# Group norm of an attention block in token order: normalised x split in halves and turned by DMA instead of x transposed on TensorE

## The reference

```python
g = v.reshape(B_, H_, W_, G, C_ // G)            # G = 32 groups of 24 channels
m = jnp.mean(g, axis=(1, 2, 4), keepdims=True)   # per image and group: 196 tokens x 24 channels
s = jnp.var(g, axis=(1, 2, 4), keepdims=True)
xn = (g - m) / jnp.sqrt(s + eps)
qkv = xn @ qkv_w.T + qkv_b                       # plus two low-rank terms in q and v
attn = softmax(q k^T / 8 + rel_h + rel_w)        # 12 heads of 64 channels
out = x + (attn v) @ proj_w.T + proj_b
```

## Time and profile before

| | |
|---|---|
| profiled execution, device time | 3388.14 us |
| its span | 3386.3 us |
| mean granted TensorE clock | 0.991 |
| PE / DVE / ACT / POOL busy | 97% / 75% / 62% / 1% |
| mean DMA traffic | 111 GB/s |

### The profile page before, as it was taken

The page is one execution under the profiler, slowest core; times in us unless marked ns, Lnnn a source line. Parts: engine busy times, 40 slices in busy tenths (PEclk is TensorE's granted clock), DMA queues, the critical chain, the costliest instruction groups (busy, mean ns, idle before and its releaser), DMA issues.

```text
span 3386.3 us, 80119 instructions
## 1 busy us (share of the span) xinstructions
PE 3295.3 (97%) x31972; PEld 2129.3 (63%) x31972; DVE 2525.2 (75%) x5966; ACT 2095.0 (62%) x5651; POOL 35.7 (1%) x65
## 2 busy tenths in 40 slices
PE   5789999999999999999999999999999999999998
PEld 3556666666666666666666666666666666666664
DVE  5677777777777777777777777777777777777764
ACT  1466666666666666666666666666666666666664
POOL 0000000000000000000000000000000000000000
PEclk9799999999999999999999999999999999999999
DMA  4145555555555565554555655556555555555555
GB/s 127 29 88 113 121 105 114 111 115 116 121 110 106 116 114 110 126 123 100 118 109 109 122 121 107 114 111 113 115 121 113 103 117 113 109 128 121 99 107 107
DMA packets 1097275, 376.13 MB, mean 111 GB/s; under 512 B 922560, under 2 KB 1077184, under 8 KB 1096904
## 3 DMA queue, kind: packets, MB, share of 16 engines
q1 hardware_dynamic: 1081070, 333.63, 50.0%
q10 hardware_dynamic: 15834, 37.37, 3.8%
HBM read 86.60 MB, written 38.54 MB: 37 GB/s over the span
## 4 chain that ended last, share of the span: by engine, by line
PE 94%; DVE 2%; ACT 1%; issue 0%; DMA 0%; POOL 0%; SPq 0%; POOLq 0%; DVEq 0%
PE ring L541 51%; PE ring L608 17%; PE score L584 9%; PE o_ps L598 7%; PE ring L563 3%; PE ring L622 3%; PE ring L614 3%; ACT prob L667 1%; PE ring L627 0%; PE ring L548 0%; DVE split L774 0%; DVE row_max L754 0%; DVE rel_sb L747 0%; DVE split L766 0%; DVE rel_sb L741 0%
## 5 line engine op out<-in xcount | busy, mean ns | idle before, releaser
L541 PE MATMUL ring<-xn_hi,w_hi 128*128 128x392 f16 x3456 | 1143.5, 331 | 4.9 <-DVE xn_lo L824 4.9
L541 PE MATMUL ring<-xn_lo,w_hi 128*128 128x392 f16 x3456 | 1140.0, 330 | 0.0
L541 PE MATMUL ring<-xn_hi,w_lo 128*128 128x392 f16 x3456 | 1139.8, 330 | 0.0
L667 ACT ACTIVATE prob<-score,neg_max,exp_scale 98x196 f32<-98x196 f32 x1536 | 768.6, 510 | 253.2 <-DVE neg_max L758 245.7
L754 DVE TENSOR_REDUCE row_max<-score 98x4 f32<-98x784 f32 x384 | 373.2, 972 | 275.1 <-PE score L584 274.1
L774 DVE SCALAR_TENSOR_TENSOR split<-prob,row_inv,split 98x196 f16<-98x196 f32 x1536 | 545.1, 418 | 7.8
L541 PEld LDWEIGHTS ring<-xn_hi,w_hi 128*128 128x128 f16 x3456 | 342.3, 99 | 260.9 <-issue 8.4
L541 PEld LDWEIGHTS ring<-xn_hi,w_lo 128*128 128x128 f16 x3456 | 338.8, 98 | 237.0 <-issue 2.6
L541 PEld LDWEIGHTS ring<-xn_lo,w_hi 128*128 128x128 f16 x3456 | 339.0, 98 | 208.8 <-issue 2.5
L608 PE MATMUL ring<-o_hi,w_hi 128*128 128x392 f16 x1152 | 380.2, 330 | 1.4 <-DVE o_lo L783 1.4
L608 PE MATMUL ring<-o_lo,w_hi 128*128 128x392 f16 x1152 | 379.6, 330 | 0.0
(11 more groups left out here) (115 smaller groups left out, 4895.7 us busy)
## 6 DMA issues: line engine op xcount, KB each, us to landing
y_sb<-in_x SPq DMA_DIRECT2D x192, 196.0 KB
out<-y_sb SPq DMA_DIRECT2D x192, 196.0 KB
x_sb<-in_x ACTq DMA_DIRECT2D x31, 1176.0 KB
rel_q<-rel_sb SPq DMA_DIRECT2D x128, 122.5 KB, 2.3
stage<-in_L_conv_qkv_w SPq DMA_DIRECT2D x3, 2304.0 KB, 19.9
turned<-split SPq DMA_TRANSPOSE x384, 4.1
rel_q<-rel_sb SPq DMA_DIRECT2D x128, 24.5 KB, 1.9
v_tok<-v_split SPq DMA_TRANSPOSE x192, 3.4
```

The costliest lines, as they stand in the source:

```text
L541: last = T.matmul(ring[:, bank, 0:NT], w[:, c, 128 * j:128 * j + 128], xx[:, par, c, :], start=(c == 0 and part == 0), stop=(c == CT - 1 a ...
L667: last = A.activation(prob[:, head, half, :], score[0:HALF, head, TOK * half:TOK * half + TOK], ACT.Exp, bias=neg_max[:, k % 2, i:i + 1], ...
```

## The change

The norm is computed on `x_sb` in token order. VectorE sums each group of 24 channels (A, two halves: one image each), one G step averages over tokens by products with a constant 98x98 matrix (four products of 64 columns, f32), B subtracts the mean in place, ScalarE squares (U), VectorE sums the squares (D), a second G gives the variance, POOL the power of -0.5 on 128 values per partition, H multiplies in place. I and L write the high and the low part to `xs` (f16, tokens on partitions), and four DMA transposes a pair (XT) write `xn`, channels on partitions, with 112 rows for 98 tokens. The buffer `xs` also serves as `squares` and as the column copy of q, so all of its zeroing is at the start. X and M are gone, weights are turned without the stride of six, `yT` has one buffer, `y_sb` two, and the lists are written anew.

```diff
-GP = C // GROUPS // CT
+GP = C // GROUPS
...
-YS = 3
+YS = 2
...
 PE_ORDER = (
-    each("S", 0, 0) + each("P", 1, 10) + each("Z", 2, 5) + each("X", -1, 3, 4, 5) + each("V", 0, 0)
-    + each("S", 0, 1) + each("P", 1, 11) + each("K", 0, 1) + each("Y", 1, 0) + each("G", -1, 0)
-    + each("S", 0, 2) + each("P", 0, 0) + each("G", -1, 1) + each("V", 0, 1) + each("Y", 1, 1) + each("Z", 1, 0)
...
+    each("S", 0, 0) + each("P", 1, 10) + each("Z", 2, 5) + each("V", 0, 0) + each("K", 0, 1)
+    + each("S", 0, 1) + each("P", 1, 11) + each("G", -1, 1) + each("V", 0, 1) + each("Y", 1, 0)
+    + each("S", 0, 2) + each("P", 0, 0) + each("K", 0, 2) + each("Y", 1, 1) + each("Z", 1, 0)
+    + each("S", 0, 3) + each("P", 0, 1) + each("Y", 1, 2) + each("Z", 1, 1) + each("V", 0, 2)
+    + each("S", 0, 4) + each("P", 0, 2) + each("Z", 1, 2) + each("K", 0, 3) + each("Q", -1, 0)
+    + each("S", 0, 5) + each("P", 0, 3) + each("V", 0, 3) + each("Q", -1, 1)
+    + each("S", 0, 6) + each("P", 0, 4) + each("K", 0, 4) + each("Q", -1, 2)
+    + each("S", 0, 7) + each("P", 0, 5) + each("V", 0, 4) + each("Q", -1, 3)
+    + each("S", 0, 8) + each("P", 0, 6) + each("G", -2, 0) + each("Q", -1, 4, 5)
+    + each("S", 0, 9) + each("P", 0, 7) + each("K", 0, 5) + each("R", -1, 0) + each("Y", 1, 3) + each("R", -1, 1)
     + each("S", 0, 10) + each("P", 0, 8) + each("R", -1, 2, 3, 4) + each("V", 0, 5) + each("Y", 1, 4) + each("Z", 1, 3)
-    + each("S", 0, 11) + each("P", 0, 9) + each("K", -1, 0) + each("X", -2, 0, 1, 2) + each("Y", 1, 5) + each("Z", 1, 4))
+    + each("S", 0, 11) + each("P", 0, 9) + each("K", -1, 0) + each("Y", 1, 5) + each("Z", 1, 4))
...
 ACT_ORDER = (
-    each("Y", 2, 5) + each("X", -1, 3) + each("N", 0, 0) + each("X", -1, 4, 5) + each("T", 0, 0)
...
-    + each("X", -2, 0, 1, 2))
+    each("Y", 2, 5) + soft(0) + each("V", 0, 0)
+    + each("K", 0, 1) + each("P", 1, 11) + soft(1) + each("V", 0, 1)
+    + each("Y", 1, 0) + each("I", -1, 0) + each("N", 0, 2) + each("K", 0, 2) + each("T", 0, 2) + each("I", -1, 1)
+    + each("Y", 1, 1) + each("P", 0, 1) + soft(3) + each("Y", 1, 2)
+    + each("V", 0, 2) + soft(4) + each("K", 0, 3)
+    + each("Q", -1, 0) + each("P", 0, 3) + soft(5) + each("V", 0, 3) + each("LD", -2, 0)
+    + each("Q", -1, 1) + each("N", 0, 6) + each("K", 0, 4) + each("T", 0, 6)
+    + each("Q", -1, 2) + each("P", 0, 5) + soft(7) + each("V", 0, 4)
+    + each("Q", -1, 3) + soft(8) + each("Q", -1, 4)
+    + each("Q", -1, 5) + each("P", 0, 7) + each("N", 0, 9) + each("K", 0, 5) + each("T", 0, 9) + each("R", -1, 0)
+    + each("Y", 1, 3)
+    + each("R", -1, 1, 2) + each("N", 0, 10) + each("R", -1, 3, 4) + each("T", 0, 10) + each("V", 0, 5)
+    + each("Y", 1, 4) + each("U", -2, 0) + each("P", 0, 9) + each("N", 0, 11) + each("K", -1, 0) + each("T", 0, 11)
+    + each("U", -2, 1))
...
 DVE_ORDER = (
-    each("S", 0, 0) + each("Z", 2, 4) + each("X", -1, 3) + each("N", 0, 0) + each("T", 0, 0) + each("Z", 2, 5)
-    + each("X", -1, 4)
...
+    each("S", 0, 0) + each("Z", 2, 4) + soft(0) + each("V", 0, 0) + each("Z", 2, 5) + each("D", -1, 1)
+    + each("S", 0, 1) + each("G", -1, 1) + each("K", 0, 1) + each("P", 1, 11) + soft(1) + each("V", 0, 1)
+    + each("H", -1, 0)
+    + each("S", 0, 2) + each("H", -1, 1) + each("N", 0, 2) + each("K", 0, 2) + each("T", 0, 2) + each("L", -1, 0)
+    + each("S", 0, 3) + each("Z", 1, 0) + each("P", 0, 1) + each("L", -1, 1) + soft(3)
+    + each("S", 0, 4) + each("V", 0, 2) + each("Z", 1, 1) + soft(4) + each("K", 0, 3)
+    + each("S", 0, 5) + each("Z", 1, 2) + each("Q", -1, 0) + each("P", 0, 3) + soft(5) + each("V", 0, 3)
+    + each("S", 0, 6) + each("Q", -1, 1) + each("N", 0, 6) + each("K", 0, 4) + each("T", 0, 6) + each("A", -2, 0)
+    + each("S", 0, 7) + each("Q", -1, 2) + each("P", 0, 5) + soft(7) + each("V", 0, 4) + each("A", -2, 1)
+    + each("S", 0, 8) + each("Q", -1, 3) + each("G", -2, 0) + soft(8) + each("Q", -1, 4) + each("B", -2, 0)
+    + each("S", 0, 9) + each("Q", -1, 5) + each("P", 0, 7) + each("N", 0, 9) + each("K", 0, 5) + each("T", 0, 9)
+    + each("R", -1, 0)
+    + each("S", 0, 10) + each("R", -1, 1, 2) + each("N", 0, 10) + each("R", -1, 3, 4) + each("T", 0, 10) + each("V", 0, 5)
     + each("S", 0, 11) + each("Z", 1, 3) + each("P", 0, 9) + each("N", 0, 11) + each("K", -1, 0) + each("T", 0, 11)
-    + each("X", -2, 0, 1, 2))
+    + each("B", -2, 1) + each("D", -2, 0))
...
 SP_ORDER = (
     each("ST", 2, 4) + each("CB", 0, 0) + each("T", 0, 0)
+    + each("VT", 0, 0) + each("ST", 2, 5) + each("LY", 1, 0) + each("T", 0, 1)
+    + each("VT", 0, 1) + each("LY", 1, 1) + each("XT", -1, 0) + each("T", 0, 2)
+    + each("XT", -1, 1, 2) + each("ST", 1, 0) + each("XT", -1, 3) + each("T", 0, 3) + each("LY", 1, 2)
+    + each("VT", 0, 2) + each("ST", 1, 1) + each("T", 0, 4) + each("LY", 1, 3)
+    + each("ST", 1, 2) + each("T", 0, 5) + each("VT", 0, 3) + each("LY", 1, 4)
+    + each("T", 0, 6)
+    + each("T", 0, 7) + each("VT", 0, 4)
     + each("T", 0, 8)
+    + each("T", 0, 9)
     + each("CA", -1, 0) + each("T", 0, 10)
+    + each("VT", 0, 5) + each("ST", 1, 3) + each("T", 0, 11) + each("LY", 1, 5))
...
-            step(G.memset(gmean[:, :], 1.0 / GP))
...
+            step(G.memset(gmean[:, :], 1.0 / (GP * TOK)))
...
+        xs = S("xs", [128, 2, 4, C], F16)
+        xn = S("xn", [128, 2, 2, 4, CT, ROWS], F16)
...
+        squares = xs[0:HALF].rearrange("p a b c -> p (a b c)").bitcast(F32).rearrange("p (b c) -> p b c", b=4)
...
-        yT = S("yT", [128, 2, NT], F32)
+        yT = S("yT", [128, NT], F32)
...
+        sums = S("sums", [HALF, 4, GROUPS], F32)
+        mean = S("mean", [HALF, 4 * GROUPS], F32)
+        var_eps = S("var_eps", [HALF, 4 * GROUPS], F32)
+        rstd = S("rstd", [HALF, 4 * GROUPS], F32)
+        minus_half = S("minus_half", [HALF, 4 * GROUPS], F32)
...
+                elif kind == "XT":
+                    part, image = k // 2, k % 2
+                    wait(sp, xs_lo_made if part else xs_hi_made, 2 * p + image + 1)
+                    sp.sem_inc(sp_go, 1)
+                    sp.dma_start_transpose(xn[:, p % 2, part, 2 * image:2 * image + 2].rearrange("p b c r -> p (b c) r"),
+                                           xs[0:ROWS, part, 2 * image:2 * image + 2].rearrange("r b c -> r (b c)")
+                                           ).then_inc(xn_in, 16)
...
-                    wait(sp, y_out[k % YS], 32 * p + 16 * (k // YS))
+                    wait(sp, y_out[k % YS], 16 * (CT // YS) * p + 16 * (k // YS))
...
-                        if kind == "Q" and k == 0 and c % 2 == 0:
-                            wait(pe, xn_lo_made, 3 * p + c // 2 + 1)
-                        for part, (w, xx) in enumerate(((w_hi, xn_hi), (w_hi, xn_lo), (w_lo, xn_hi))):
+                        if kind == "Q" and k == 0 and c == 0:
+                            wait(pe, xn_in, 64 * p + 64)
+                        for part, (w, xx) in enumerate(((w_hi, 0), (w_hi, 1), (w_lo, 0))):
                             last = T.matmul(ring[:, bank, 0:NT], w[:, c, 128 * j:128 * j + 128],
+                                            xn[:, par, xx, :, c, 0:HALF], start=(c == 0 and part == 0),
...
-                elif kind == "X":
-                    if k == 0:
-                        wait(pe, x_in, 16 * p + 16)
-                    for i in range(4):
-                        src = x_sb[:, i, :].rearrange("p (a b) -> p b a", b=CT)[:, k, :]
-                        last = T.transpose(ring[:, bank, HALF * i:HALF * i + HALF], src, ident[0:HALF, 0:HALF])
...
-                    wait(pe, group_in, 2 * p + k + 1)
-                    src = mean_var[:, :, 0] if k == 0 else spread[:, :]
-                    T.matmul(ring[:, bank, 0:2], gmean[:, :], src, start=True, stop=True).then_inc(done[kind], 1)
+                    wait(pe, summed, 4 * p + 2 * k + 2)
+                    out = ring[0:HALF, bank, 0:4 * GROUPS].rearrange("p (n b g) -> p n b g", n=2, b=2)
+                    of_half = sums[:, :, :].rearrange("p (n b) g -> p n b g", n=2)
+                    for to in range(2):
+                        for image_half in range(2):
+                            last = T.matmul(out[:, :, to], gmean[:, :], of_half[:, :, image_half],
+                                            start=(image_half == 0), stop=(image_half == 1))
+                    last.then_inc(done[kind], 1)
...
+                        wait(act, xs_lo_made, 2 * p)
...
-                    A.activation(yT[:, k % 2, :], ring[:, bank, 0:NT], ACT.Identity,
+                    wait(act, done["Z"], 6 * p + k)
+                    A.activation(yT[:, :], ring[:, bank, 0:NT], ACT.Identity,
                                  bias=bias[:, 3 * CT + k:3 * CT + k + 1],
                                  scale=y_scale[:, :]).then_inc(read["Y"], 1)
...
+                elif kind == "U":
+                    wait(act, centred, 2 * p + k + 1)
+                    wait(act, done["R"], RCH * p)
                     two = slice(2 * k, 2 * k + 2)
```

(47 more changed lines are left out.)

125 lines of the change are left out of this document (21 added, 104 removed).

## The result

The changed kernel takes 3918.7 us (median of four runs, 3916.3 to 3919.4) against 3388.0 us for the kernel before on the same chip: 15.6% slower, ratio 1.1565 [1.1547, 1.1582]. The profiled execution has a span of 3917.3 us and a device time of 3919.1 us. The forecast was 3411 us, in a range of 3340 to 3640.

A forecast was written before the change was run, and what follows sets the result against it. PE was taken to bound the kernel, 97% busy. From 3388.1 us, 31 periods gain 0.1 us each, the start adds 23 and the end 3: 3411 us, own range 3385 to 3445, full range 3340 to 3640.

The forecast's parts named there:

- The power: POOL's power for 128 values per partition, before H0: taken as 3 us, bounds 0.69 and 44 us, hidden up to 4.5 us.
- its cover on DVE: DVE's other work (K1, P11, softmax of unit 1, V1) before H0, said to hide the power up to 4.5 us.
- The power outlasts its cover: Rival at H on DVE: from 4.5 us every us costs 31; 8 us gives 3524, 44 us 4680; chance 0.33.
- PE's list: PE's work per period: 100.47 less 3.18 for X and 0.46 for old G, plus 1.3 for new G, 98.1 us.
- G's eight records: Each new G step's f32 products on PE: 0.08 us a record, 0.65 us a step, 1.3 us a period.
- The products over broken runs: L541's products on PE read four runs of 98 columns instead of one of 392, and P's broken runs: priced at 0.
- The walk from S11 to G1: PE stalls 2.15 us at Z5 for ACT's Y5 behind U1, then 0.1 us at G1 for D1: 2.25 us a period.
- the forecast's own period: Steady period on PE: 98.1 us of work plus 2.25 us of stall, 100.4 us.
- The start: Path to the first Q: more zeroing, then norm steps and XT 3 taking 29 us instead of 11.5; together +23 us.
- PE stays the bound: Rival at Z5: Y5 is not late, 2.35 us a period gained, 3341 us; chance 0.11.
- XT and T in one queue at no cost: XT's four transposes a pair beside T's twelve in SP's queue: 4.1 us landing hidden, nothing added in the steady part.

The follow-up runs named there:

- short_power: Changed kernel with POOL's power on 2 of its 128 columns, the other columns of rstd left at 1: 3467.6 us, ratio 1.0232.
- y5_first: short_power with ScalarE's Y5 put in front of U1 instead of behind it: 3470.5 us, ratio 1.0243.
- The best order found: newton64 with reordered engine lists, the load of x issued earlier, transfers of xs respaced and pads awaited at first use: 3370.1 us, ratio 0.9945.
- no_stall: short_power with G0 a stretch earlier, A and B in the slots of products 5 to 8, x loaded two stretches earlier: 3430.9 us, ratio 1.0118.
- newton64: Changed kernel with 64 columns instead of 128 and the power replaced by a bit guess and three Newton steps on POOL: 3438.2 us, ratio 1.0150.

## Why the prediction was wrong

The step that failed is "The power", the term "I take 3 us". It measured 20.77 us, 16.4 us beyond its cover on DVE, and that alone takes the time out of the range. Of its two bounds, 0.69 and 44 us, I took a value next to the lower one, since the other POOL rows cost nanoseconds an element. But those rows are of other operations (a fill, a select), and the only row of a power has two columns, and how much of its 0.69 us is fixed could not be read from it, as the text said itself. The runs say 0.37 us fixed and 0.32 for the two columns. The chance of a power over 11.6 us was put at 0.15, and the range left it out; with no row that separates the fixed part from the part per column, the range had to reach the 44 us or the case needed more weight.

The mechanism was named and its arithmetic held:
- "The power outlasts its cover: from 4.5 us on every us costs 31." The cover on DVE measured 4.4 us. At 20.77 us the rival's own sum is 3411 + 31 x 16.3 + 18 = 3934 us; 3918.7 was measured. That it comes this near is partly luck, since errors in it cancel: DVE's wait of 16.4 us arrives at PE as 12.7 (31 x 3.7 = 115 us less), and the lower clock behind the waits (about 2.6 us a period) and a G of 0.85 us (0.4) give some 90 us of that back.
- PE's list: forecast 98.1 us; short_power's period less its waits and its time at the lower clock gives 98.4. G's eight records take 0.85 us, not 0.65. The products over broken runs cost nothing, as forecast: the median record is 0.327 us long, before 0.329 (they overlap; 18 take 2.98 us as before).
- The walk from S11 to G1: PE waits 2.2 us at Z5 for Y5 (forecast 2.15). At G1, where 0.1 us was forecast, it does not wait: D1 ends 0.95 us sooner than PE gets there in short_power, 0.3 us sooner in the period of the changed kernel above. y5_first shows that it is one lateness with two places.
- A second step failed, the cost of these waits. A wait was counted as its length, and the forecast's own period of 100.4 us would have been 102.4 (short_power): 0.4 from G, and some 1.6 from the clock. So even with a power of 0.69 us the time is 3468, not 3409, outside the forecast's own range of 3385 to 3445.
- The start: forecast +23 us, measured +41; less the 17.8 us that the power was longer than forecast it is 23.
- "PE stays the bound", with 2.35 us a period gained and 3341 us, did not happen in this order. The best order found, whose list is another 0.85 us shorter, gains 1.6 us a period.
- XT and T in one queue at no cost: right for the change (L592 waits for turned 4.0 us in all), since PE came late. In no_stall the transfers of xs were the next thing late, 1.5 us a period, but there the load of x had been moved beside them.

On the power I had weighed the Trainium skill, GPSIMD Engine Reference, section 3.1, whose rate for a two-input elementwise instruction gave 1.0 us by my estimate. The trace of newton64 has plain two-input operations of 64 columns at 0.29 to 0.36 us, which does not speak against that rate; the power of the same 64 columns takes 10.55 us. The rate does not hold for that function, and the measurement decides.
